# Local attention: the norm matmuls moved from the end of a slot to behind the next slot's scores, with the orders of ScalarE and VectorE to match, and the first gate in the transposes' bank

## The reference

```python
for i in range(DEPTH):                                   # 6
    x = attn_layer(shift_tokens(x), Wqkv[i], ...) + x    # 16 heads of 64, windows of 32
    x = ffn_layer(shift_tokens(x), ...) + x              # gated, 128 -> 2*341 -> 128

def attn_layer(x, Wqkv, qs, ksc, Wo):
    q, k, v = heads of x @ Wqkv
    q = l2norm(q) * qs ; k = l2norm(k) * ksc
    q = q * cos * scale + rotate_half(q) * sin * scale
    k = k * cos / scale + rotate_half(k) * sin / scale
    out = local_attention(q, k, v)       # softmax over the own and the previous window
    return out @ Wo

def ffn_layer(x, g, bln, W1, b1, W2, b2):
    a, gate = split((layernorm(x) * g + bln) @ W1 + b1)
    return a * gelu(gate) @ W2 + b2
```

## Time and profile before

| | us |
|---|---|
| median of 2 runs | 2795.55 (2792.01 to 2799.09) |
| profiled execution, its own time | 2792.94 |
| its span | 2791.1 |
| first to last score matmuls (192 slots) | 106.0 to 2234.8 |
| busy, share of the span | TensorE 83%, VectorE 71%, ScalarE 59%, GpSimd 39% |
| TensorE idle before the norm matmuls (L483), until the DMA `cross<-sq` landed | 293.3 in 147 waits |
| ScalarE idle before L662, until those matmuls | 275.8 in 149 |

### The profile page before, as it was taken

How to read it: one execution, slowest core, us unless ns; L and a number is a source line. 1 busy time by engine, 2 the same in 40 slices (tenths; PEclk the granted TensorE clock), 3 DMA queues, 4 the chain that set the end, 5 groups by cost and what they waited for, 6 DMA issues and landing times. The chain is left out here.

```text
span 2791.1 us, 66156 instructions
## 1 busy us (share of the span) xinstructions
PE 2330.5 (83%) x25708; PEld 1181.8 (42%) x25708; DVE 1975.9 (71%) x2597; ACT 1641.4 (59%) x2401; POOL 1081.2 (39%) x461
## 2 busy tenths in 40 slices
PE   7688888888888888888888888888888878777778
PEld 2244444444444444444444444444444432222355
DVE  5567777777767777777767777777767638999642
ACT  4456666666666666666666666666666646545633
POOL 0343444344443444444443444344443402556220
PEclk8899999999999999999999999999999989999979
DMA  0211111111111111111111111111111110000001
GB/s 21 68 28 25 24 39 43 32 24 28 36 36 37 27 28 36 36 32 36 24 36 36 32 36 24 24 47 36 32 24 24 24 35 0 0 0 0 17 16 45
DMA packets 46741, 80.26 MB, mean 29 GB/s; under 512 B 9760, under 2 KB 12208, under 8 KB 46384
## 3 DMA queue, kind: packets, MB, share of 16 engines
q1 hardware_dynamic: 46480, 76.14, 10.8%
HBM read 24.73 MB, written 1.05 MB: 9 GB/s over the span
## 5 line engine op out<-in xcount | busy, mean ns | idle before, releaser
L753 POOL TENSOR_TENSOR f_shuf<-f_shuf,f_tabs 128x1024 f32<-128x1024 f32 x192 | 451.9, 2354 | 1292.4 <-DVE f_shuf L791 1292.4
L483 PE MATMUL f_ps<-f_sq,f_same 64*64 64x512 f32 x768 | 220.5, 646 | 293.8 <-DMA f_cross<-f_sq 293.3
L757 POOL TENSOR_TENSOR f_rot<-f_rot,f_shuf 128x1024 f32<-128x1024 f32 x192 | 452.8, 2359 | 27.5
L662 ACT ACTIVATE f_rn<-f_ps 128x1024 f32<-128x1024 f32 x192 | 197.2, 1027 | 276.0 <-PE f_ps L483 275.8
L814 DVE TENSOR_REDUCE f_max<-f_ps 128x8 f32<-128x512 f32 x192 | 132.6, 691 | 253.2 <-PE f_ps L506 251.2
L528 PEld LDWEIGHTS f_ps<-f_ptz,f_v 64*64 64x64 f32 x6144 | 259.7, 133 | 93.5 <-issue 93.5
L528 PE MATMUL f_ps<-f_ptz,f_v 64*64 64x96 f32 (+1 forms) x6144 | 286.1, 243 | 1.9 <-ACT f_ptz L675 1.6
L791 DVE STREAM_SHUFFLE f_shuf<-f_ps 128x1024 f32<-128x1024 f32 x192 | 249.5, 1299 | 0.3
L656 ACT ACTIVATE f_sq<-f_ps 128x1024 f32<-128x1024 f32 x192 | 195.0, 1016 | 92.7 <-PE f_ps L471 91.9
L805 DVE SCALAR_TENSOR_TENSOR f_qk<-f_rn,f_rot 128x1024 f32<-128x1024 f32 x192 | 233.6, 1217 | 21.2 <-POOL f_rot L757 13.1
L798 DVE TENSOR_TENSOR f_rot<-f_ps,f_tabc 128x1024 f32<-128x1024 f32 x192 | 231.7, 1207 | 0.0
(11 more groups left out here) (266 smaller groups left out, 3989.3 us busy)
## 6 DMA issues: line engine op xcount, KB each, us to landing
f_cross<-f_sq SPq DMA_DIRECT2D x384, 128.0 KB, 2.3
e_w<-in_e_w SPq DMA_DIRECT2D x16, 256.0 KB, 2.8
f_wq<-in_f_wq SPq DMA_DIRECT2D x12, 256.0 KB, 2.7
f_wk<-in_f_wk SPq DMA_DIRECT2D x12, 256.0 KB, 3.4
f_wv<-in_f_wv SPq DMA_DIRECT2D x12, 256.0 KB, 3.5
f_wo<-in_f_wo SPq DMA_DIRECT2D x6, 512.0 KB, 3.3
f_w<-in_f_w SPq DMA_DIRECT2D x6, 341.0 KB, 3.0
s_dx<-in_k_pick SPq DMA_DIRECT2D x1, 1536.0 KB, 9.0
```

The lines of the kernel that those rows point to most:

```text
L483: mm = pe.matmul(view(ps, NBANK[h] * CH, [1, CH], p0=64 * (h if own else 1 - h), rows=64), same_head[k, k], of, start=True, stop=True, ski ...
L753: pool.tensor_tensor(view(shuf, 0, [S, 4], [1, S]), view(shuf, 0, [S, 4], [1, S]), view(tab_s, 0, [S, 2], [0, 2], [1, S]), ALU.mult).then_ ...
L757: pool.tensor_tensor(rot[:, :], rot[:, :], shuf[:, :], ALU.add).then_inc(sem["rot"], 1)
```

## The change

TensorE's `norms` is now called for pair j+1 right behind `scores(j)` (behind the output projection in slot 2 and behind the gates in slot 6) and before `project(j+2)`; before it was called for pair j+2 at the end of the slot. `inverse_norm` is split: ScalarE's `norm_log(j+1)` comes ahead of the softmax exponential of pair j, and `norm_exp(j+1)` right behind it. VectorE runs `soft_b(j)` ahead of `normalise(j+1)`, `tables` and `hidden(1)`. The first gate goes to bank 2, where the transposes are: it now waits for `ptz` (the spread of the last transposes), the transposes of slot 6 wait for its gelu, and `values` no longer does. No instruction is added or removed, and no shape changes.

```diff
--- before.py
+++ after.py
@@ -337,7 +337,7 @@
         bank = lambda k, n=1: view(ps, k * CH, *([[CH, n]] if n > 1 else []), [1, CH])
 
         Y0, H0_, G0 = NU, 1, 1
-        GBANK = (6, 0, 1)
+        GBANK = (2, 0, 1)
         NBANK = (6, 7)
 
 
@@ -448,8 +448,6 @@
                 need(pe, sem[f"wv{q // 4}"], (i // NU) * 16 + 16)
                 need(pe, sem["v"], i * 8 + q)
                 need(pe, sem["ln"], i * 8 + q)
-                if q == 0:
-                    need(pe, sem["gelu"], i * 3 - 6 + 1 + G0)
                 for r in range(2):
                     for h in range(2):
                         at = 128 * (q % 4) + 64 * r
@@ -511,6 +509,8 @@
             def turn(i, j):
                 need(pe, sem["p"], i * 8 + j + 1)
                 need(pe, sem["ptz"], i * 8 + j)
+                if j == 5:
+                    need(pe, sem["gelu"], i * 3 - 3 + 1 + G0)
                 for t in range(4):
                     mm = pe.transpose(view(ps, 2 * CH + 128 * t, [1, 128]), s[j % 2][:, 128 * t:128 * t + 128], ident[:, :])
                 mm.then_inc(sem["t_mm"], 1)
@@ -578,6 +578,7 @@
                 k = i - 1
                 has, u, a = (run, i, j + 2) if j < 6 else (more, i + 1, j - 6)
                 had1, u1, b1 = (run, i, j - 1) if j >= 1 else (before, k, 7)
+                next1, u3, a3 = (run, i, j + 1) if j < 7 else (more, i + 1, 0)
                 had2, u2, b2 = (run, i, j - 2) if j >= 2 else (before, k, j + 6)
                 if run:
                     scores(i, j)
@@ -589,6 +590,8 @@
                     need(pe, sem["straight"], i * 8 + 8 if run else 0)
                     gate_mm(k, 1)
                     gate_mm(k, 2)
+                if next1:
+                    norms(u3, a3)
                 if j == 6 and had2:
                     mix(u2, b2)
                 if has:
@@ -609,14 +612,11 @@
                     hid_mm(k, 2)
                 if had1:
                     turn(u1, b1)
-                if has:
-                    norms(u, a)
                 if before and j == 4:
                     variance(k)
                 if before and j == 5:
                     hid_mm(k, 0)
-                    if run:
-                        need(pe, sem["ln"], i * 8 + 8)
+                    need(pe, sem["ptz"], i * 8 + 5 if run else i * 8)
                     gate_mm(k, 0)
                 if before and j == 7:
                     w2_mm(k)
@@ -655,12 +655,15 @@
                 need(act, sem["n_mm"], i * 8 + j)
                 act.activation(view(sq, 0, [UNIT, 2], [1, UNIT]), bank(0, 2), ACT.Square).then_inc(sem["sq"], 1)
 
-            def inverse_norm(i, j):
+            def norm_log(i, j):
 
                 need(act, sem["n_mm"], i * 8 + j + 1)
                 need(act, sem["qk"], i * 8 + j)
                 act.activation(view(rn, 0, [UNIT, 2], [1, UNIT]), bank(NBANK[0], 2), ACT.Ln,
                                scale=float(2.0 ** 20)).then_inc(sem["ln"], 1)
+
+            def norm_exp(i, j):
+
                 need(act, sem["ln"], i * 8 + j + 1)
                 act.activation(rn[:, :], rn[:, :], ACT.Exp, scale=-0.5, bias=con.lift).then_inc(sem["rn"], 1)
 
@@ -698,10 +702,14 @@
                     gelu(k, 1)
                     gelu(k, 2)
                     nc.scalar.preload_act_table_set(ACT_SET)
+                if next1:
+                    norm_log(u3, a3)
                 if run:
                     need(act, sem["shift"], i * 8 + j + 1)
                     act.activation(view(ps, 4 * CH, [CH, 2], [64, 4], [1, 64]), view(s[j % 2], 0, [64, 2], [128, 4], [1, 64]),
                                    ACT.Exp, scale=8.0).then_inc(sem["exp"], 1)
+                if next1:
+                    norm_exp(u3, a3)
                 if has:
                     square(u, a)
                 if before and j == 4:
@@ -716,8 +724,6 @@
                     out_copy(u2, b2)
                 if had1:
                     spread(u1, b1)
-                if has:
-                    inverse_norm(u, a)
                 if before and j == 4:
                     need(act, sem["var"], k + 1)
                     act.activation(sq2[:, :], bank(3), ACT.Ln, bias=con.eps).then_inc(sem["ln2"], 1)
@@ -850,14 +856,14 @@
                     hidden(k, 0)
                 if before and j == 7:
                     hidden(k, 2)
+                if run:
+                    soft_b(i, j)
                 if next1:
                     normalise(u1, a1)
                 if j == 6 and more:
                     tables(i + 1)
                 if before and j == 6:
                     hidden(k, 1)
-                if run:
-                    soft_b(i, j)
                 if has:
                     shuffle(u, a)
                     straight(u, a)
```

## The result

The changed kernel takes 2889.45 us (median of 2 runs, 2887.62 to 2891.28) against 2795.55 before: the ratio is 1.034, 95% interval 1.027 to 1.040. It is slower by 94 us where 55 to 58 us less were forecast, and outside the range of 2685 to 2800. The span of the profiled execution is 2885.8 us. The difference lies in the 192 slots. Their first and last score matmuls stand at 98.6 and 2332.5 us, before at 106.0 and 2234.8: the slots take 105 us more, 7.4 us are gained ahead of them and about 3 behind.

The account below looks back on a forecast made before the run. Round trips through ScalarE and VectorE, including the squares' DMA, were taken as the bound. A unit of 87.3 instead of 89.76 us, plus 0.3 for the clock, gave 50 us, the first unit 5: 2738, range 2685 to 2800.

Parts of the forecast that it names:

- The walk: Lump-by-lump timing of one full unit, slots 0 to 7, in the new order: 87.3 us instead of 89.76.
- about cancel: Slots 6 and 7: their changes in length were said to about cancel, against 3.2 us won in slot 5.
- the term for the clock: Allowance of 0.3 us a unit for idle stretches like those of slot 6 lowering TensorE's clock.
- a rival the clock: Clock falls behind idle stretches in slots 3, 6 and 7, up to 1.7 us each: 2855 us; chance 0.08.
- the rival with 0.2: VectorE's product (L878 before) is held by GpSimd's second pass, slot 5's maximum 2.6 us later: 2798; chance 0.2.
- the two rivals: The clock falling more often (chance 0.08) and the product held by GpSimd's second pass (chance 0.2).
- the moved norms add nothing to TensorE's work: TensorE's work stays 74 to 75 us a unit after the norms move.
- its DMA wait: Slot 5: the 3.39 us wait for the squares' DMA and the low clock go; slot falls from 14.1 to about 11.
- The rival of shorter round trips: Slot 2, or slots 4 and 5: ScalarE delays hidden, 2.4 us less in each place, 2683 for one; chance 0.17.

Follow-up runs that it names:

- The second experiment: Changed kernel with the exponential written to PSUM, so VectorE's product L884 reads only one SBUF tensor: 2834.33 us, ratio 1.015.
- e1: Changed kernel plus filler matmuls of constants in TensorE's idle stretches (slots 3 to 7), results unread: 2778.39 us, ratio 0.992.
- e5: Changed kernel with both the filler matmuls and the second factor of product L884 in PSUM: 2779.52 us, ratio 0.994.
- e6: e5 plus, in slots 0 to 2, ScalarE's softmax exponential ahead of the logarithm of the norms: 2771.31 us, ratio 0.989.
- e9: Changed kernel, no fillers, L884's factor in PSUM, two waits at the norms, slots 6 and 7 ordered projection, values, mix: 2765.26 us, ratio 0.990.
- The fastest kernel: e9 plus fillers in slots 3, 4 and 7 and, in slot 2, the softmax exponential ahead of the logarithm: 2656.07 us, ratio 0.949.

## Why the prediction was wrong

**The walk's lengths held.** Where the clock stays up, the slots came out as walked. From the scores of slot 2 to the maximum of slot 3 it said 15.1 us, measured 15.20 (1150.33 to 1165.53); from there to the maximum of slot 4 it said 9.1, measured 9.07; from the maximum of slot 5 to slot 6 it said 7.8, measured 7.68 (1186.24 to 1193.92). Slot 6 was to take 12.25 and takes 12.32 at full clock. The maximum of slot 4 to that of slot 5 is where the walk broke, 9.15 said and 11.64 measured. With the fillers the whole kernel takes 2778, 40 us above the walk's 2738, and that stands in slots 0 and 1 (21.2 us instead of 19.8) and slot 7 (15.25 instead of 14.1), not between them. The walk's own sum is told loosely in one place: slots 6 and 7 do not "about cancel", they lengthen the unit by 0.95 against unit 10. And the earlier trace rows have the transposes at 0.66, not 0.53.

**The step that failed is the term for the clock**: 0.3 us a unit, where the fillers win back 5.0 (94.7 to 89.7). As a rival the clock had a chance of 0.08 and a price of up to 117 us. It costs 111. I had the place right (idle stretches of 2.3, 2.6 and 1.9 us in slots 3, 6 and 7; measured 2.17 before slot 4, 2.34 in slot 6, 0.89 and 1.23 in slot 7) and put 0.3 us a unit on them, because in unit 10 only 3.39 us lowered the clock. I saw that the mean of the earlier trace rows lay 0.46 above unit 10 and took that for what such stretches would go on costing, instead of asking how often they did it. In 5 units of the trace of before the clock also fell around slot 7, behind an idle stretch of about 2.05 us at the end of slot 6. Unit 12 is one of them (the norms at the end of its slot 6, then its slot 7 as a stretch):

```profile
1249.07 0.65 PE L483 MATMUL f_ps<-f_sq,f_same 64*64 64x512 f32 x2 [2.06 <-DMA f_cross<-f_sq]
```

```profile
1250.09:1264.60 14.51, 12.43 (x135) 6.27 (x132) 8.74 (x13) 8.99 (x12) 6.20 (x3) 0.88 0.17 44
```

A stretch of two microseconds did it in 5 of 22 units there. In the changed kernel stretches of about 2.2 and 2.34 us do it in 18 and 20 of 22 units. What makes the difference between 5 and 18, the runs do not show. The Trainium skill says in TensorE: Matmul & The Clock Gate, section What's actually happening, that the gate goes by how busy the engine has been recently. The experiments agree: filler matmuls alone bring 111 us, and the granted clock of the 22 units goes from 0.93 to 0.99.

**L884 missed its gap**, the rival with 0.2, but as a consequence of the first. Where the clock stayed up it lasts 1.31: held 0.6 until the first pass ends, as the walk had it. Where slot 4 ran at half speed the square had to wait for its projection, L884 came later, was 0.24 us late for its gap and was held 2.0 us (the rival said 2.6). The second experiment gives about 40 us to taking it away altogether. SBUF — State Buffer, section Who interferes with whom, in the Trainium skill had named the case that no row of before showed, and here the measurement agrees with it. I had given the two rivals chances as if they were independent; one sets off the other.

**A term was missing**: the waits of the norms behind the scores, 0.34 to 0.5 us in slots 0 and 1. Before, the norms of these slots stood behind transposes and output matmuls and had no idle time ahead of them. In the changed kernel they have none in slots 2 and 6 either, where they stand behind the output and gate matmuls, with the same four waits. Behind the 64 short score matmuls it is 0.54 us, and 0.15 with two waits. So TensorE's queue gets through the waits under longer matmuls and not under these. I wrote that the moved norms add nothing to TensorE's work. The same goes for the end of a unit: the last projection starts 4.17 us before the next scores (1218.76 to 1222.93) where I took 3.37 from the earlier trace rows. TensorE is idle for 1.32 us of that ahead of the first masks of the pass; over the passes it is 1.26 in the median, before 0.44. The last projection now has to wait itself (0.51 us), and I take it that the loop's jump is no longer hidden behind queued work, but no run tests that.

**What was right.** Slot 5 did lose its DMA wait, and its low clock in all but 3 units, though it takes 11.97 us and not about 11; the gate's part was free, slots 0 and 1 gained nothing, and slot 2's exponential came 5.2 us behind its scores. The rival of shorter round trips (0.17) did not occur.

**How the loss is made up.** With fillers on both sides the new order is worth nothing (2778 against 2769). The loss is then the clock that falls 2.8 times a unit instead of 1.2 times, and what hangs on it. What stays open is why the falls in slot 0 come in 6, 10 or 16 of 22 units as slots 3 and 5 get shorter (e1, e5, e6), with the work around slot 0 unchanged. Of the changed kernel itself no version with moved code was run, but it shows no stall like e9's and has the 242 instruction packets of the kernel before.

## What to carry to other kernels

Do not count only the idle time that a reordering removes: list the idle stretches that it creates on TensorE and ask for each whether the clock may fall behind it. Do not take the shortest one that lowered it in one unit for a limit: here stretches of 2.05 us did it in 5 of 22 units and of 2.34 in 20 of 22, and in the fastest kernel the clock still falls in 12 of the slots 0, where TensorE is idle for 1.0 to 1.8 us in most units. A fall mostly cost 1.3 to 1.9 us of its slot. Filler matmuls are a cheap test, and sometimes the remedy. A chain that is walked lump by lump gives lengths to a few tenths of a microsecond, but an instruction that has to slip in between two passes of another engine by 0.6 us should be taken as held. And a stall that nothing in the profile releases is worth a look at the instruction packets on the page, and a run with a few idle instructions ahead of the loop. A remedy found on the changed kernel should be tried on the kernel before as well, or it says little about the change.

## What the hardware showed that was not expected

- A row of 128x512 with two SBUF operands on VectorE lasts 2.66 us when it starts 0.24 us behind a GpSimd pass of 2.35 us, and 0.69 us when one operand is in PSUM, under the same pass.
- Four pairs of wait and increment on TensorE cost 0.54 us of idle time behind short matmuls, two pairs 0.15.
- TensorE stalled 2.1 to 2.6 us behind each of the loop's 21 jumps back in one kernel, which fetched 21 instruction packets more, and not at all at this place when 24 or 48 idle instructions stood ahead of the loop. A comparison of two kernels whose code differs can be off by that, here by 78 us in 2765.
- The fastest kernel, 2656 us, does ten matmuls a unit more than the work needs.
